# Three pairs of PSUM banks that rotate between score and maximum rounds in the first attention of a two-layer block

## The reference

```
xn = layernorm(x)
Q, K, V = relu(xn @ Wq + bq), relu(xn @ Wk + bk), relu(xn @ Wv + bv)   # 16 heads of 8
scores = Q K^T / sqrt(8); masked where the key's sum is 0 and above the diagonal
attn = softmax(scores); out = attn V, times the query's mask
s = gamma * normalise(out + xn) + beta
x = x + s * silu(ffn(xn))
```

## Time and profile before

| | |
|---|---|
| median of 3 runs | 3488.9 us (3487.67 to 3503.65) |
| profiled execution: its own time | 3474.64 us |
| span from first to last instruction | 3472.6 us, 65333 instructions |
| TensorE busy | 2886.7 us (83%) |
| VectorE busy | 2281.3 us (66%) |
| ScalarE busy | 1491.3 us (43%) |
| GpSimd busy | 1242.1 us (36%) |
| mean granted TensorE clock | 0.923 of 2.4 GHz |
| first attention, exponentials | from 458.2 us on, the last starts at 1331.3 |

### The profile page before, as it was taken

The page is one execution under the profiler, slowest core; times in us unless marked ns, Lnnn a source line. Parts: engine busy times, 40 slices in busy tenths (PEclk is TensorE's granted clock), DMA queues, the critical chain, the costliest instruction groups (busy, mean ns, idle before and its releaser), DMA issues. The chain is left out here.

```text
span 3472.6 us, 65333 instructions
## 1 busy us (share of the span) xinstructions
PE 2886.7 (83%) x21249; PEld 1834.7 (53%) x21249; DVE 2281.3 (66%) x5750; ACT 1491.3 (43%) x2383; POOL 1242.1 (36%) x1379
## 2 busy tenths in 40 slices
PE   0035488888898984899999999999999977999999
PEld 0023233333333332566666666666666656888888
DVE  8978367787777773566666666666666646555555
ACT  3434335444444443444544444544444532222322
POOL 4546402121212211455555555555555540000000
PEclk9987579889898887899999999999999998999999
DMA  1000122222222111011101111111111012010100
GB/s 49 0 6 0 51 77 71 84 66 77 71 74 86 60 49 43 17 36 36 35 26 35 35 35 32 33 32 35 35 35 35 29 34 64 24 36 24 36 24 25
DMA packets 157089, 143.52 MB, mean 41 GB/s; under 512 B 33313, under 2 KB 125026, under 8 KB 156899
## 3 DMA queue, kind: packets, MB, share of 16 engines
q1 hardware_dynamic: 156912, 141.66, 13.3%
HBM read 88.22 MB, written 42.86 MB: 38 GB/s over the span
## 5 line engine op out<-in xcount | busy, mean ns | idle before, releaser
L1644 DVE CUSTOM_DVE_ANT_0 a_scored<-a_pMax,a_causal 128x128 bf16<-128x128 f32 (+3 forms) x1024 | 451.8, 485 | 463.2 <-PE a_pMax L1768 463.2
L1005 DVE TENSOR_REDUCE a_max<-a_pMax 128x2 f32<-128x1024 f32 (+3 forms) x512 | 403.4, 820 | 217.9 <-PE a_pMax L624 115.1
L939 ACT ACTIVATE a_PT<-a_pST 128x1024 f32<-128x1024 f32 (+1 forms) x384 | 338.6, 882 | 385.2 <-PE a_pST L624 239.9
L1561 ACT ACTIVATE a_PT<-a_pST 128x1024 f32<-128x1024 f32 (+1 forms) x384 | 338.9, 882 | 380.9 <-PE a_pST L1758 366.6
L1510 POOL TENSOR_SCALAR_AFFINE_SELECT a_PT<-a_PT 128x256 f32<-128x256 f32 x512 | 202.9, 408 | 642.5 <-ACT a_PT L1561 611.9
L2047 ACT ACTIVATE m_silu<-m_pG 128x512 f32<-128x512 f32 x256 | 153.3, 599 | 411.4 <-PE m_pG L2139 411.4
L1776 PE MATMUL a_pO<-a_PT,a_V 128*64 128x512 f32 (+3 forms) x2048 | 324.7, 462 | 0.7 <-POOL a_PT L1510 0.7
L2147 PEld LDWEIGHTS m_pY<-m_w,m_hT 128*128 128x128 f32 x2048 | 248.0, 191 | 9.9
L872 POOL TENSOR_TENSOR a_att<-a_att,a_rows 128x512 f32<-128x512 f32 x16 | 20.2, 1264 | 643.4 <-DVE a_att L1066 643.4
L2094 DVE TENSOR_TENSOR m_hT<-m_pU,m_silu 128x512 f32<-128x512 f32 x256 | 176.9, 691 | 110.2 <-PE m_pU L2139 91.7
L2147 PE MATMUL m_pY<-m_w,m_hT 128*128 128x128 f32 x2048 | 248.8, 275 | 0.0
(11 more groups left out here) (283 smaller groups left out, 6626.2 us busy)
## 6 DMA issues: line engine op xcount, KB each, us to landing
a_rden<-inverse_sums_dram SPq DMA_DIRECT2D x256, 128.0 KB, 2.9
a_KS<-k_parts_dram SPq DMA_DIRECT2D x64, 224.0 KB
a_QS<-q_parts_dram SPq DMA_DIRECT2D x64, 192.0 KB
a_xn_staged<-xn SPq DMA_DIRECT2D x32, 256.0 KB, 3.1
a_max_rows<-a_mT SPq DMA_DIRECT2D x512, 2.0 KB
q_parts_dram<-a_parts SPq DMA_DIRECT2D x16, 384.0 KB, 2.6
k_parts_dram<-a_parts SPq DMA_DIRECT2D x16, 384.0 KB
ln_x<-in_L_attn_x SPq DMA_DIRECT2D x8, 512.0 KB, 7.2
```

The lines of the kernel that those rows point to most:

```text
L939: a.activation(PT[p][:, :, at:at + w], pST[:, :, 0:w], ACT.Exp, scale=SCALE).then_inc(exped.sem, 1)
L1005: last = v.tensor_reduce(MX[:, :, p, j], pMax[(NM * p + m) % 2][:, :, at:at + (j + 1) * P], AX.X, ALU.max, negate=True)
L1561: a.activation(PT[s.q % 2][:, :, k * TOK:k * TOK + w], pST[:, :, 0:w], ACT.Exp, scale=SCALE).then_inc(exped.sem, 1)
L1644: last = v.tensor_tensor_reduce(scored[:, cc, at:at + w], pMax[:, cc, at:at + w], causal[:, TOK - w:], -1.0, 3e38, ALU.add, ALU.min, MX[pa ...
```

## The change

The three pairs of banks are named alike and given out in the order in which TensorE issues the rounds: score, maximum, score, maximum. Since that order has two rounds to each k and the pairs number three, every round takes the pair of the third round before it, which is always one of the other kind. Score round k of a pair uses pair 2k mod 3, maximum round m uses pair (2m + 1) mod 3. So score round n now waits for the reduction of maximum round n + 16 (the one issued three rounds before), and maximum round n + 18 for exponential n - 1. In the first 18 maximum rounds, which stand alone, a maximum round waits for reduction n - 3; in the score rounds from 368 on, which stand alone too, score round n waits for exponential n - 3. No instruction of an engine is added or removed; the number of semaphore waits is the same.

```diff
+    AHEAD = NM * LEAD
...
-        pMax = [ps(f"pMax{i}", [P, 2, TOK]) for i in range(2)]
-        pST = ps("pST", [P, 2, TOK])
+        banks = [ps(f"pair_banks{i}", [P, 2, TOK]) for i in range(3)]
+        score_bank, max_bank = [banks[2 * k % 3] for k in range(NS)], [banks[(2 * m + 1) % 3] for m in range(NM)]
...
-                a.activation(PT[p][:, :, at:at + w], pST[:, :, 0:w], ACT.Exp, scale=SCALE).then_inc(exped.sem, 1)
+                a.activation(PT[p][:, :, at:at + w], score_bank[k][:, :, 0:w], ACT.Exp, scale=SCALE).then_inc(exped.sem, 1)
...
-                    last = v.tensor_reduce(MX[:, :, p, j], pMax[(NM * p + m) % 2][:, :, at:at + (j + 1) * P], AX.X, ALU.max, negate=True)
+                    last = v.tensor_reduce(MX[:, :, p, j], max_bank[m][:, :, at:at + (j + 1) * P], AX.X, ALU.max, negate=True)
...
             def max_round(u, par, pair, p, m):
                 n = NM * (PAIRS * u + p) + m
-                bank = pMax[(NM * p + m) % 2]
-                maxed.wait(pe, n - 2)
+                bank = max_bank[m]
+                if isinstance(n, int) and n <= AHEAD:
+                    maxed.wait(pe, n - 3)
+                else:
+                    exped.wait(pe, n - AHEAD - 1)
...
             def score_round(u, par, pair, p, k):
-                exped.wait(pe, NS * (PAIRS * u + p) + k - 1)
+                n = NS * (PAIRS * u + p) + k
+                if isinstance(n, int) and n - 2 + AHEAD >= NM * PAIRS * NU:
+                    exped.wait(pe, n - 3)
+                else:
+                    maxed.wait(pe, n - 2 + AHEAD)
```

More of the change, by code:

```diff
@@ L1191, in score_round @@
                         rows = split_rows(half)
-                        pe.matmul(pST[:, half, at:at + TOK - kb * P], KS[par][rows, pair, kb * P:(kb + 1) * P],
+                        pe.matmul(score_bank[k][:, half, at:at + TOK - kb * P], KS[par][rows, pair, kb * P:(kb + 1) * P],
                                   QS[par][rows, pair, kb * P:TOK], start=(at == 0), stop=False)
                 for half in range(2):
-                    mm = add_far(pe, pST[:, half], [at for at, _ in ROUNDS[k]], far, identb)
+                    mm = add_far(pe, score_bank[k][:, half], [at for at, _ in ROUNDS[k]], far, identb)
                 mm.then_inc(st_ready.sem, 1)
```

## The result

The kernel after takes 3473.3 us (median of 8 runs, 3462.1 to 3478.8), the kernel before 3492.8 (8 runs, 3482.7 to 3507.4): ratio 0.9936, 95% interval 0.9911 to 0.9962. Run again beside other kernels it gave 0.9963 (0.9942 to 0.9984). So it is faster by about half a per cent: 16 to 20 us by the medians, 13 to 22 by the ratios. The forecast was 3486, no change; the time lies in its range, 3468 to 3512. The two profiled executions hardly differ (3472.6 and 3473.0 us of span), which is no contradiction: the one of before, 3474.64 us, lies 8 us under the fastest of the eight runs of its kernel.

What follows compares the result with a forecast made beforehand. Each batch was taken as bound by VectorE for 32.0 us and by PE for 22.8. Terms of -10.3 + 12.0 + 5.7 - 2.0 + 0.0 - 1.0 - 7.0 = -2.6 gave 3472, 3486 on the median's scale; range 3468 to 3512.

Steps and rivals of the forecast that it cites:

- No change: Outcome within about 0.5%, 17 us, of the kernel before, from 3471 to 3506; chance 0.67.
- What goes: Score rounds in PE's stretch of batches 1 to 13 stop waiting for the exponential just before: -10.3 us.
- A: Rival: second slow clock period in every batch, 3522, chance 0.12. As part: score round 0 to first reduction behind k=8.
- Exit: Score round k = 21, where VectorE's stretch ends: PE leaves one score round, 0.92 us, late per batch; +12.0 us.
- the delay handed to GpSimd: PE's lateness at k = 12 and 13 reaches GpSimd, which blocks VectorE: 0.44 us a batch, +5.7 us.
- B: Rival: 4 batches lose their second slow clock period, 3470, chance 0.12. As part: that reduction to score round 21.
- Middle: Batches 1 to 13: stalls that go, late exit and handed delay together, -10.3 + 12.0 + 5.7 us.
- C: Rival: a reduction starves at k = 12 or 13, +18, 3505, chance 0.10. As part: score round 21 to next batch.
- End: Score rounds after the last maximum rounds wait for the third exponential back, -7; k = 3 to 5 of batch 15, -1.0.
- Batch 14: Stalls saved and the late exit come out even, 0.46 + 0.47 against 0.84: 0.0 us.
- Start: The 18 opening maximum rounds with three bank pairs, 1.0 us left at score round 0, and batch 0: -2.0 us in all.
- D: Rival: the exponential was the bound and VectorE's stretch follows PE, so 39.4 + 8.9 us come back, 3441; chance 0.06.

Runs made afterwards that it cites:

- the closed end: The kernel after, but its last 16 score rounds each wait for the exponential just before them, as in the kernel before: 3483.0 us, ratio 0.9987.
- before again: The kernel before, unchanged, run and profiled a second time: 3490.9 us, ratio 1.0003.
- longer code: The kernel before with one more wait, for a reduction long done, in each score round of the loop: 3510.7 us, ratio 1.0060.
- the short reductions: Reductions over a quarter of one block row: kernel before 3414.2 us (0.980), full rotation with the shorter register arithmetic 3372.2 us (0.968).

## Why the prediction was right, and where it was not

The form was right: two waits of like size, of which only the ones in PE's stretch can be earned, paid for at the exit of VectorE's stretch, and an end of the stage that gains. "No change" was the likeliest case at 0.67; what came, 0.4 to 0.6 per cent faster, lies on that case's edge. That the profile's own 3475.04 us for the kernel after stands so near to the sum's 3472 is luck: the ends gave more than forecast, and the execution that the sum starts from had fewer disturbances than most. Step by step:

- **What goes, -10.3.** Right. In batches without a disturbance A is 18.7 or 18.9 us long against 19.5 or 19.7 before: 0.85 a batch, 11 in all. Nothing reappears at the maximum rounds.
- **Exit, +12.0, and the delay handed to GpSimd, +5.7.** Right in sum, in part by luck: B grew from 359.9 to 374.7, 376.9 and 378.0 us, by 14.8 to 18.1, against 17.7. But an undisturbed B is only 1.1 us longer (28.7 and 29.0 in turn, against 27.6 and 27.9), and 14.8 is the profile in which none is disturbed; the others have one or two B of 30.1 or 31.4 us. The exit is the 0.92 us forecast. The handed delay was taken too high: from the reduction behind k = 8 to the blocked instruction of piece 1 it is 881.05 - 865.55 = 15.50 us, against 764.48 - 749.19 = 15.29 before, so 0.2 us a batch and not 0.44. The coupling is there as stated: L1046 and L1051 last 1.08 and 1.04 us and end with the GpSimd operations begun at 880.95 and 883.52. The rule that the prediction gives from the Trainium skill ("SBUF — State Buffer", section on the two separate sides) goes on holding for L1051, which has two inputs; L1046 has one, so that part of the rule doesn't speak of it, and the rows again show it blocked.
- **Middle, +7.4 in sum.** Five profiles of the old loop at its own length give 725.1 to 749.3, mean 737.0; three of the kernel after 742.7 to 743.4, mean 743.0: +6.0. That agrees, but the old loop scatters by 24 us, so these means can't tell +7.4 from nothing. They also hide two terms that I did not have. One is PE's stalls at the loop's jumps: C 104.2 against a mean of 96.0. The other is in A, 280.5 to 262.2, of which 11 are the stalls that the first term took away. In those five profiles 26 of 65 A's last 23 us or more, with 8 to 13 us at 1.2 GHz; in the three of the kernel after (one of them with the closed end) 1 of 39 does. VectorE's stalls lie in A and PE's in C, so a part of this is only moved from one to the other.
- **End, -7 and -1.0: the term that was too small.** Both lie in batch 15, which went from 44.8 and 43.2 to 31.7 us, by 11.5 to 13.1. What was left out is the clock. Windows of batch 15 in the kernel before, before again and after, with columns as in the earlier trace rows:

```profile
1287.12:1331.94 44.82, 34.64 (x286) 12.33 (x285) 21.01 (x83) 23.21 (x29) 5.07 (x4) 0.85 0.05 14
```
```profile
1306.27:1349.47 43.20, 32.22 (x286) 11.80 (x285) 20.82 (x83) 23.20 (x29) 5.06 (x4) 0.92 0.05 14
```
```profile
1297.53:1329.18 31.65, 28.75 (x285) 11.31 (x285) 21.45 (x85) 22.30 (x29) 5.08 (x4) 1.00 0.07 19
```

  PE's idle time falls from 10.2 and 11.0 us to 2.9: by 7.3 to 8.1, as the two terms had it. But the same matmuls also take less time, 28.75 us in place of 34.64 and 32.22, with the granted share up from 0.85 and 0.92 to 1.00: another 5.9 and 3.5 us. In batch 15 TensorE spent 13.7 us at 1.2 GHz in the first profile, 6.8 in the second, none after; half of that is what a busy engine would lose, 6.8 and 3.4 us. The closed end agrees: with 3.4 us at 1.2 GHz and 9.9 idle it took 40.7.
- **Batch 14, 0.0.** Wrong by the same omission: 52.1 to 47.5. Its A went from 23.5 to 18.7 us: 17.1 us of the batch were at 1.2 GHz in both profiles of before, 3.4 after. The one profile of the old waits that had 3.4 there by chance (longer code) took 48.2.
- **Start, -2.0.** -1.5 to -2.3 at score round 0 (forecast 1.0: PE at 1.2 GHz was less in the way than read) and about -0.5 in batch 0 (forecast 1.0).
- **Rivals.** B was the one that counts in part: fewer second half-rate periods, at the ends in each profile and in the middle by tendency only. A and C did not happen, though batches of 58 us and more did come more often than four times, six in the first profile after: they stand at the loop's jumps, with a stall or with a slow A behind it, and not for the reason of A; DVE's waits for maximum rounds inside its stretch stay at semaphore size. D is refuted by B's length and by the short reductions. What I had not named is that the one profile was a favourable execution of the kernel before, so that a sum against its own time understates a gain that consists of removing disturbances.

What stays open: why the short code is fetched again at some jumps and not at others, why VectorE stalls where it isn't, and what decides whether a second half-rate period follows. For the last only tendencies are shown.

## What to carry to other kernels

Two waits at one shared resource are worth loosening only in the stretches in which the engine that waits is the bound; find those stretches per batch, and price the other wait at the point where the bound changes hands, for one round's length there is the whole cost. Look at the ends of a pipeline by themselves: where one kind of work runs out, its buffers lie idle, and here 16 rounds given the free banks brought most of the gain of a rotation through 384. And a stall on TensorE can have two prices, its length and the clock after it, as batch 15 shows. Last, a single profile is one execution out of a scatter: compare its time with the unprofiled runs before a sum starts from it.

## What the runs showed of the hardware

- A loop of some 1700 TensorE instructions a turn has a stall of 2 to 5 us at each of its five jumps back, on TensorE or on VectorE, in each of the twelve profiles. TensorE has it when nine packets of 16 KB move on the instruction queue in that turn, VectorE when none do. 35 to 41 register instructions more on TensorE (before 118 in the program) made all five TensorE's in three profiles and four of five in a fourth. 41 of them, with the waits that they serve, cost 0.6 per cent in the old schedule.
- A VectorE operation of 0.16 or 0.17 us on 4 elements a partition, L1046 or L1051, takes up to 1.08 us when a GpSimd operation on 512 elements has begun just before it; it ends with that one.
- The granted clock varies between executions of one program: in batches 1 to 13 of the kernel before 174 and 208 us at 1.2 GHz in two profiles, with 725 and 745 us of time.
